# Last layer of a four-layer graph network: 64-column products, vectors scaled by ScalarE, edge weights four tiles at a time

## The reference

```
m_s, m_v = s_src[src] + s_dst[dst], v_src[src] + v_dst[dst]
w = rbf @ W_rbf                                  # 16 -> 224 edge weights
f_s, f_v = cg(m_s, m_v, y0, y1, w)               # first tensor product
alpha    = (leaky(f_s @ W_alpha) * alpha_dot).sum()
val_s, val_v = f_s @ Ws_val, f_v @ Wv_val        # "values"
val_v    = val_v * sigmoid(val_s @ Wg)
g_s, g_v = cg(silu(val_s), val_v, y0, y1, w2)    # second tensor product
out_s, out_v = g_s @ Ws_vlin, g_v @ Wv_vlin      # last linear map

# cg, for scalars s, vectors v, y0 (1 number), y1 (3 numbers) of the edge:
#   scalars: w_ss*s*y0,  w_vv0*dot(v, y1)/sqrt(3)
#   vectors: (w_sv*s) y1,  w_vs*v*y0,  w_vv1*cross(v, y1)/sqrt(2)
```

## Time and profile before

| | us |
|---|---|
| two runs | 7532.61 and 7553.23, median 7542.92 |
| profiled execution | 7540.86 |
| its span, first to last instruction | 7539.1 |

### The profile page before, as it was taken

One profiled execution on the slowest core, in us unless ns is written; L12 is line 12 of the kernel. 1 busy time (PEld: TensorE's weight loads), 2 busy tenths in 40 slices (PEclk: granted clock), 3 DMA queues, 4 the chain that ended last, 5 costly groups with the idle time before them and its releaser, 6 DMA issues. The chain is left out here.

```text
span 7539.1 us, 114096 instructions
## 1 busy us (share of the span) xinstructions
PE 6856.3 (91%) x33212; PEld 4573.4 (61%) x33212; DVE 6220.2 (83%) x17049; ACT 3780.0 (50%) x10162; POOL 4659.6 (62%) x3462
## 2 busy tenths in 40 slices
PE   6999999997899999989999998599999999999488
PEld 3454454545454454454444545488888888888376
DVE  6999999986677777757777777599999999998884
ACT  3555555543233222232322333377777777777485
POOL 2888888872566666526666662477777777775000
PEclk7999999996889999879999998799999999999697
DMA  8999999996222222212222220344444444444263
GB/s 226 177 178 176 175 178 175 177 170 161 57 55 56 55 56 57 49 29 58 59 57 60 58 59 23 88 97 97 95 99 96 98 97 97 98 96 87 86 189 90
DMA packets 549605, 770.78 MB, mean 102 GB/s; under 512 B 96449, under 2 KB 401126, under 8 KB 548742
## 3 DMA queue, kind: packets, MB, share of 16 engines
q0 software_dynamic: 317376, 413.42, 33.7%
q1 hardware_dynamic: 227382, 349.43, 15.1%
q10 hardware_dynamic: 4240, 0.64, 0.1%
HBM read 462.23 MB, written 300.92 MB: 101 GB/s over the span
## 5 line engine op out<-in xcount | busy, mean ns | idle before, releaser
L704 POOL DMA_INDIRECT fore<-node_table,src_i x1616 | 1709.1, 1058 | 963.1 <-issue 473.2
L1659 DVE TENSOR_TENSOR work<-work 128x384 f32<-128x384 f32 (+4 forms) x4885 | 1999.4, 436 | 63.0 <-DMA work<-src_sum 26.9
L814 POOL DMA_INDIRECT fore<-src_table,put_i x784 | 1359.0, 1733 | 449.1 <-ACT fore L1145 268.1
L771 POOL DMA_INDIRECT src_sum<-work,put_i x808 | 1283.3, 1588 | 401.1 <-issue 184.2
L1402 PE MATMUL bank<-work 128*128 128x384 f32 (+1 forms) x3232 | 1315.0, 555 | 97.8 <-DVE work L1659 86.6
L1402 PEld LDWEIGHTS bank<-work 128*128 128x128 f32 x3232 | 650.3, 212 | 850.1 <-issue 387.4
L973 ACT ACTIVATE work<-bank 64x512 f32<-64x512 f32 x404 | 239.0, 591 | 1788.3 <-PE bank L1369 1052.7
L1659 DVE TENSOR_TENSOR work<-work,bank 128x385 f32 (+4 forms) x2056 | 889.5, 433 | 173.9 <-remote 71.8
L1383 PE MATMUL bank<-w_fc,work 64*128 64x192 f32 x3232 | 660.6, 346 | 112.4 <-issue 81.4
L1383 PEld LDWEIGHTS bank<-w_fc,work 64*128 64x128 f32 x3232 | 536.4, 194 | 360.3 <-issue 323.0
L1354 PE MATMUL bank<-work 128*128 128x480 f32 x1616 | 746.3, 595 | 2.1 <-DVE work L1659 1.9
(11 more groups left out here) (280 smaller groups left out, 12742.3 us busy)
## 6 DMA issues: line engine op xcount, KB each, us to landing
edge_h<-work SPq DMA_DIRECT2D x196, 320.0 KB
work<-edge_h SPq DMA_DIRECT2D x196, 320.0 KB, 3.4
work<-keys SPq DMA_DIRECT2D x196, 256.0 KB
fore<-in_dst_row SPq DMA_DIRECT2D x196, 256.0 KB
fore<-node_table,src_i POOLq DMA_INDIRECT x1616
work<-in_edge_attr SPq DMA_DIRECT2D x196, 128.0 KB
src_sum<-work SPq DMA_DIRECT2D x4, 6240.0 KB, 40.7
work<-src_sum SPq DMA_DIRECT2D x100, 240.0 KB, 4.7
```

The source lines that it names most:

```text
L704: return pool.indirect_dma_start(dst, None, table, bass.IndirectOffsetOnAxis(ap=idx, axis=0), bounds_check=bound, oob_is_err=True)
L771: pool.indirect_dma_start(src_sum[t], bass.IndirectOffsetOnAxis(ap=put_i[:, e:e + 1], axis=0), E.run[:, g % 2, t * 480:(t + 1) * 480], Non ...
L814: pool.indirect_dma_start(T.rows[:, b, t, :], None, src_table, bass.IndirectOffsetOnAxis(ap=put_i[:, e:e + 1], axis=0), compute_op=ALU.add ...
L1659: return V_.tensor_tensor(o, p, q, op)
```

## The change

It touches only the first pass of the last layer.

- The weight matrices `lin_x` and `lin_yz` get 64 columns each and lose their zeros; each product starts and stops its own 64 columns.
- DVE's product of `vv` with y0 goes. ACT makes it: four scaled copies of 96 elements for each group (`vectors_by_y0`), with two new signals, `vv_ready` (DVE to ACT) and `vv_by_y0` (ACT to PE and DVE).
- PE makes the edge weights of all four tiles of a group in even h and nothing in odd h; they lie side by side in the two banks. ACT copies the unscaled ones of four tiles in one instruction in odd h.

```diff
-        weight("lin_x", 128, 128)
-        weight("lin_yz", 128, 128)
+        weight("lin_x", 128, 64)
+        weight("lin_yz", 128, 64)
...
                 def weights_by_y0_3(h):
                     b, at = h // 2 % 2, h % 2 * 2
-
-                    act.wait_ge(s.w3_mm, h + 1)
+                    if at == 0:
+
+                        act.wait_ge(s.w3_mm, h // 2 + 1)
                     for t in range(2):
-                        act.activation(T.w[:, b, at + t, 0:96], bank[:, t, 0:96], ACT.Copy,
+                        act.activation(T.w[:, b, at + t, 0:96], bank[:, t, at * 112:at * 112 + 96], ACT.Copy,
                                        scale=y[:, h * 2 + t:h * 2 + t + 1, 0])
                 def other_weights(h):
-                    b, at = h // 2 % 2, h % 2 * 2
-                    act.activation(T.w[:, b, at:at + 2, 96:224], bank[:, 0:2, 96:224], ACT.Copy).then_inc(s.w3_out, 1)
+                    b, g = h // 2 % 2, h // 2
+                    if h % 2 == 0:
+                        return
+                    act.activation(T.w[:, b, :, 96:224].rearrange("p (a t) c -> p t a c", t=2),
+                                   bank[:, 0:2, 0:448].rearrange("p t (a c) -> p t a c", c=224)[:, :, :, 96:224],
+                                   ACT.Copy).then_inc(s.w3_out, 1)
...
+                def vectors_by_y0(h):
+                    if h % 2:
+                        return
+                    g = h // 2
+                    b = g % 2
+
+                    act.wait_ge(s.vv_ready, g + 1)
+                    for t in range(GROUP):
+                        last = act.activation(T.f2[:, b, t, 160:352].rearrange("p (i c) -> p i c", c=64)[:, :, 0:V], T.vv[:, t], ACT.Copy,
+                                              scale=y[:, g * GROUP + t:g * GROUP + t + 1, 0])
+                    last.then_inc(s.vv_by_y0, 1)
...
-                                      (0, m2_turned), (-3, by_y0), (-6, other_weights), (-6, turns), (-9, dst_rows_out)])
+                                      (0, m2_turned), (-3, by_y0), (-1, vectors_by_y0), (-6, other_weights), (-6, turns), (-9, dst_rows_out)])
...
                 def edge_w3(h):
-                    g, b, at = h // 2, h // 2 % 2, h % 2 * 2
-                    if at == 0:
-
-                        pe.wait_ge(s.rbf_in1 if b else s.rbf_in0, 32 * (g // 2 + 1))
-                    if h:
-
-                        pe.wait_ge(s.w3_out, h)
-                    for t in range(2):
-                        rows = slice(32 * t, 32 * t + 16)
-                        last = nc.tensor.matmul(bank[:, t, 0:224], T.rb[rows, b, at * 64:at * 64 + P],
+                    g, b = h // 2, h // 2 % 2
+                    if h % 2:
+                        return
+
+                    pe.wait_ge(s.rbf_in1 if b else s.rbf_in0, 32 * (g // 2 + 1))
+                    if g:
+
+                        pe.wait_ge(s.w3_out, g)
+                    for t in range(GROUP):
+                        rows, c0 = slice(32 * (t % 2), 32 * (t % 2) + 16), t // 2 * P
+                        last = nc.tensor.matmul(bank[:, t % 2, t // 2 * 224:(t // 2 + 1) * 224], T.rb[rows, b, c0:c0 + P],
                                                 wt["rbf"][rows], start=True, stop=True)
                     last.then_inc(s.w3_mm, 1)
...
                         pe.wait_ge(s.m2_done, h // 2 + 1)
 
+                        pe.wait_ge(s.vv_by_y0, h // 2 + 1)
+
...
-                        nc.tensor.matmul(o[:, 64:192], t2[:, t, 128:256], wt["lin_x"][:], start=True, stop=False)
-                        last = nc.tensor.matmul(o[:, 64:192], t2[:, t, 256:384], wt["lin_yz"][:], start=False, stop=True)
+                        nc.tensor.matmul(o[:, 64:128], t2[:, t, 128:256], wt["lin_x"][:], start=True, stop=True)
+                        last = nc.tensor.matmul(o[:, 128:192], t2[:, t, 256:384], wt["lin_yz"][:], start=True, stop=True)
...
-                    dve.wait_ge(s.w3_out, 2 * g + 2)
+                    dve.wait_ge(s.w3_out, g + 1)
...
+                    if g:
+
+                        dve.wait_ge(s.vv_by_y0, g)
                     tt(vv, bc(cv[:, :, 68:100], 2, 3), bc(ys[:, :, 0:3], 3, V), ALU.mult).then_inc(dve_own, c.step())
...
-                    tt(vv, vv, bc(f[:, :, 64:96], 2, 3), ALU.mult).then_inc(dve_own, c.step())
-                    dve.wait_ge(dve_own, c.n - 1)
+                    tt(vv, vv, bc(f[:, :, 64:96], 2, 3), ALU.mult).then_inc(s.vv_ready, 1)
+                    dve.wait_ge(dve_own, c.n)
...
-                    tt(vsl[:, :, :, 0:V], vv, y0_planes(yy), ALU.mult).then_inc(dve_own, c.step())
-                    dve.wait_ge(dve_own, c.n - 1)
+                    dve.wait_ge(dve_own, c.n)
```

More of the change, by code:

```diff
@@ L261, in build @@
             "rbf_in0", "rbf_in1", "w3_mm", "w3_out", "m1_done", "m1_turned", "m1_in_sbuf", "values_mm",
-            "sigmoid_out", "values_read", "values_out", "m2_done", "m2_turned", "m2_in_sbuf", "linear_mm", "linear_out",
+            "sigmoid_out", "values_read", "values_out", "vv_ready", "vv_by_y0", "m2_done", "m2_turned", "m2_in_sbuf", "linear_mm", "linear_out",
             "h_done", "h_kept0", "h_kept1",
@@ L516, in _ @@
                 wload(wt[name + "_x"][64:128, 32:64], a[key][64:128])
-                wload(wt[name + "_yz"][0:64, 64:96], a[key][64:128])
-                wload(wt[name + "_yz"][64:128, 96:128], a[key][64:128])
+                c0 = 64 if name == "val" else 0
+                wload(wt[name + "_yz"][0:64, c0:c0 + 32], a[key][64:128])
+                wload(wt[name + "_yz"][64:128, c0 + 32:c0 + 64], a[key][64:128])
             sp.wait_ge(zero_made, 1)
@@ L624, in rbf @@
                     if g >= 2:
-                        sp.wait_ge(s.w3_mm, 2 * g - 2)
+                        sp.wait_ge(s.w3_mm, g - 1)
                     attrs = a["edge_attr_16"][:, g * 512:(g + 1) * 512].rearrange("k (t o n) -> o k t n", o=2, n=P)
@@ L2371, in m2 @@
                     dve.wait_ge(s.sigmoid_out, 2 * g + 2)
-                    tt(vv, vv, bc(f[:, :, 64:96], 2, 3), ALU.mult).then_inc(dve_own, c.step())
-                    dve.wait_ge(dve_own, c.n - 1)
+                    tt(vv, vv, bc(f[:, :, 64:96], 2, 3), ALU.mult).then_inc(s.vv_ready, 1)
+                    dve.wait_ge(dve_own, c.n)
                     tt(scores, scores, cv[:, :, 64:68], ALU.add).then_inc(dve_own, c.step())
-                    dve.wait_ge(dve_own, c.n - 1)
+                    dve.wait_ge(s.vv_ready, g + 1)
                     nine_products(vv, g)
-                    tt(vsl[:, :, :, 0:V], vv, y0_planes(yy), ALU.mult).then_inc(dve_own, c.step())
-                    dve.wait_ge(dve_own, c.n - 1)
+                    dve.wait_ge(dve_own, c.n)
                     tt(f[:, :, 64:96], nine[:, :, 0, :], nine[:, :, 1, :], ALU.add).then_inc(dve_own, c.step())
@@ L2386, in _ @@
                 vv = T.vv
-                def y0_planes(yy):
-                    return bc(yy[:, :, 0:1].broadcast_to([P, GROUP, 3]), 3, V)
                 def edge_out(g):
```

## The result

| | before | after |
|---|---|---|
| median of two runs | 7542.92 us | 8022.22 us (8011.6 and 8032.83) |
| span of the profiled execution | 7539.1 us | 8009.9 us |
| mean granted clock of TensorE over the span | 0.921 | 0.891 |

The ratio is 1.0632 with a 95% interval of 1.058 to 1.0683: slower, and by nearly twice the 257 us of the forecast. 8022 us lies outside the stated range of 7660 to 7900.

What follows compares the result with a forecast made beforehand. PE's order, with its waits for ACT's copies, was taken to bound the stage at 10.7 us a group. +1.44 and -0.10 gave +1.34 a group, times 192 +257 us on 7541: 7798 us, range 7660 to 7900.

Steps and rivals of the forecast that it cites:

- The mechanism of the forecast: Last layer, first pass: ACT's vector copies delay its weight copy and so PE's edge weights; +1.34 us a group.
- One-tile half from turns to values: Half group with one tile of destination rows, from turning the first messages to the value matmuls: +1.44 us.
- the lower bound: If the second four edge weights cost less than the first, ACT's own way takes over after 0.16 us: -0.16.
- The linear map: PE's last block in each half: 64 columns instead of 128 save 0, since weight loads set the pace.
- The two-tile half: Half group with two tiles of destination rows, losing its edge weights: -0.13 us, -0.10 on average.
- the register load: PE's sequencer loads sixteen window numbers every fourth group, 1.11 us each; it still ends last, so nothing is saved there.
- The clock falls too: Rival, 17%: PE's added idle time lowers its granted clock in the changed stage; 0.65 us a group more, 7923 us.
- A narrower stream saves nothing: Last linear map: 64 columns gain nothing behind weight loads of 128 columns; taken as 0, with nothing lost as a bound.
- The rival with DVE as the beat: Rival, 15%: DVE bounds the stage, so its removed 0.47 us come off every group; 7449 us, or 7382 with shorter linear map.
- The 7.1 us: DVE's idle time in 11 waits within 500 us of the stage, read as waiting for ACT, so DVE has slack.

Runs made afterwards that it cites:

- late vectors alone: Kernel before, with only ACT's four scaled vector copies added, issued behind its wait for the values and ahead of the weight copy: ratio 1.0188.
- early: Changed kernel with ACT's four vector copies issued ahead of its wait for the value matmuls instead of behind it: ratio 1.0002.
- the filler: Changed kernel with one unread product a group placed in PE's wait for ACT's weight copy: 7740.84 us, ratio 1.0268.
- wide products and edge weights by two: Kernel before, with ACT's vector copies added behind its wait for the values, two of the four cut in pieces: ratio 1.0411.
- the vectors early, 128 columns wide: Changed kernel with ACT's vector copies ahead of its wait for the values, edge weights two tiles at a time, products 128 columns wide: ratio 1.0005.

## Why the prediction was wrong

**The mechanism of the forecast was right, its sum too high.** ACT's late copies hold the weight copy, the weight copy holds PE's edge weights: shown by the wait L1519 <- L1139, by the late vectors alone (+0.83 us a group) and by their being free when early. The sum was +1.34 a group; with the filler, at full clock, it is +0.94. Term by term, in that run against before:

- One-tile half from turns to values: 1.83 to 3.10 us (5501.18 to 5504.28), +1.27, forecast +1.44. Eight edge weights take 0.96 to 0.98 us and not 1.16: the second pairs cost less than the first, as the lower bound had it.
- The linear map: 1.284 for 1.337 us in both halves, -0.11 a group, forecast 0. The weight load does pace it; 0.05 us of 1.34 is what halving two thirds of the columns saves.
- The two-tile half: 2.08 us before on average, register load included, 1.85 after: -0.23, forecast -0.10. I wrote that nothing is saved in the groups with the register load. In fact the sequencer comes to it 0.58 us earlier, as no edge weights stand before its rows, and the destination rows start 1.38 us after the turns and not 1.96.

These add up to +0.93. So at full clock the change costs about 184 us and not 257; this error and the next one pull in opposite ways.

**The step that failed is the clock.** "The clock falls too" had 17% and 0.65 us a group, 7923 us; it happened and cost 1.58, some 310 us, where the forecast put nothing into its sum and kept the clock at 1.00. Two errors stand in it. The chance: I set 84% busy at a clock of 1.00 against the earlier layers' 0.93, and judged by busy time. The stretch of the earlier trace rows has waits of 1.14 us as long as the new one, but with products 128 wide and no edge weights. The runs show that a wait of this length is not judged by itself: with the wide products 1.01 us gives 49 slow stretches, with the narrow ones 1.06 us gives 167, and with wide products and edge weights by two 1.17 us gives 32. The busy share does not tell it either: PE is busy 447.63 of 500 us at 0.97 with the products 128 wide, and 451.43 at 0.88 in the changed kernel, though a lower clock itself lengthens the busy time. The price: I spread a mean clock over the group and took 58% of the slow time as being on the path. But the slow stretch begins after the wait and covers most of the values and the turns, which are on the path from end to end; 3.4 us at half speed lose 1.7 us, and the fall comes in nine groups of ten.

**"A narrower stream saves nothing: nothing lost."** This was the costliest sentence. In time of its own the narrow product is nearly free either way, but undone alone it gives back 1.068 - 1.0415, some 2.7% or 200 us, through the clock (the two runs are from two chips, each against the kernel before on its own). That it could lose there was not among the bounds.

**The rival with DVE as the beat** is out: with the product gone and the vectors early, 128 columns wide, the group stays at 10.82 us, and DVE is at 469 of 500 us. The removed 0.47 us of DVE bought nothing. The 7.1 us that the prediction gives as DVE's wait for ACT are "issue" in the earlier trace rows; its conclusion, that DVE has slack, does not suffer by it.

**Open.** Which waits the clock falls at is not settled as a rule. Shown are four facts: the long wait has to be there (a product of 0.39 us in it ends the falls), work elsewhere does not replace it, a still longer wait in the kernel before brings only 32 falls in 187 groups, and narrow products and four-tile edge weights each make falls more frequent. Whether the two act by columns, by the 0.05 and 0.22 us that they add to the wait, or by when the waits come, was not taken apart.

## What to carry to other kernels

Work moved to an engine with idle time is free only if it is issued where the engine idles; look at what stands behind it in that engine's list and who waits for that. A wait of TensorE of one microsecond can cost more through the granted clock than by itself (here 1.58 us a group against 0.94): before accepting such a wait, look for the clock in the windows view, and try a filler product in it. A change that only shortens TensorE's work ahead of such a wait makes the wait longer, and is not neutral.

## What the runs showed of the hardware

- A product of 0.39 us that nobody reads, placed in a wait of 1.05 us of PE, made the whole program 4% faster (8063 to 7741 us); placed in the other half of the loop it did nothing (1.0675).
- Two runs with nearly the same busy share of PE, 451 and 448 of 500 us, had 167 and 49 slow stretches and granted clocks of 0.88 and 0.97.
- The falls of the clock follow each other at a fixed 13.65 us (147 of 166 in the changed kernel), and a loop whose group is as long as that, 13.66 us, had one in every group.
- An fp32 product is two pairs of weight load and matmul. With loads of 128 weight columns a pair costs 0.107 us in a block whose products all stream 64 columns, and 0.111 us in one where two thirds stream 128. The Trainium skill, "TensorE: Matmul & The Clock Gate", section "LDWEIGHTS (loading the stationary operand)", gives about 107 ns for such a load by its formula, and the trace agrees. The table of the same page of the Trainium skill under "Back-to-back issue gap", for matmuls alone, has 134 cycles at 128 columns; at 2.4 GHz that is an estimated 56 ns, about half of what these blocks take.
- Four edge-weight tiles in a row take 0.985 us, two take 0.578: the second two cost 0.41.
- ACT's four scaled copies of 96 elements start 0.265 us apart, as interpolated from 64 and 160 elements.
